# Second attention's tiles: two additions in a row on GpSimd, low keys on VectorE

## What is computed

```python
def _apply_rope(x):
    rot = jnp.stack((-xr[..., 1], xr[..., 0]), axis=-1).reshape(x.shape)
    return x * jnp.cos(ang) + rot * jnp.sin(ang)
...
x = x + 0.5 * ffn0(ln(x)); x = x + attn0(ln(x)); x = x + 0.5 * ffn0(ln(x))
x = x + 0.5 * moe1(ln(x)); x = x + attn1(ln(x)); x = x + 0.5 * moe1(ln(x))
# attn1: q, k, v = split(x @ W_qkv.T); q, k = rope(q), rope(k)
#        softmax(causal(q @ k.T / 4)) @ v, then @ W_o.T
```

## Time and profile before

| what | us |
|---|---|
| median of the runs (lowest, highest) | 843.3 (840.75, 847.4) |
| profiled execution, its own time | 837.3 |
| its span, first to last instruction | 835.5 |
| R of tile 0 starts; C3 is done | 555.6; 581.0 |
| R of tile 4 starts; C7 is done | 630.2; 657.3 |

### The profile page before, as it was taken

The page is one execution under the profiler, slowest core; times in us unless marked ns, Lnnn a source line. Parts: engine busy times, 40 slices in busy tenths (PEclk is TensorE's granted clock), DMA queues, the critical chain, the costliest instruction groups (busy, mean ns, idle before and its releaser), DMA issues. The chain is left out here.

```text
span 835.5 us, 17560 instructions
## 1 busy us (share of the span) xinstructions
PE 718.3 (86%) x5515; PEld 483.5 (58%) x5515; DVE 628.1 (75%) x1436; ACT 458.0 (55%) x1033; POOL 402.9 (48%) x412
## 2 busy tenths in 40 slices
PE   7898959999979999989898699855897598988985
PEld 3454437777636777755455466433785487545652
DVE  5989878778787778698987577543898596775646
ACT  3444568887757788646423266325574475324541
POOL 4545766767666676358636277424005320331440
PEclk8999989999989999999999799976799598998997
DMA  9999994000000000030001243300000010013324
GB/s 371 328 303 182 241 216 2 0 0 0 1 1 1 0 0 0 1 120 1 1 14 51 77 116 109 133 1 1 1 2 1 18 35 2 2 61 88 115 84 151
DMA packets 64945, 59.07 MB, mean 71 GB/s; under 512 B 29106, under 2 KB 59186, under 8 KB 64370
## 3 DMA queue, kind: packets, MB, share of 16 engines
q1 hardware_dynamic: 60706, 47.85, 23.5%
q0 software_dynamic: 3744, 10.26, 3.5%
q10 hardware_dynamic: 432, 0.15, 0.1%
HBM read 27.92 MB, written 30.33 MB: 70 GB/s over the span
## 5 line engine op out<-in xcount | busy, mean ns | idle before, releaser
L1504 PE MATMUL PS<-XT,WA 128*128 128x512 f16 x432 | 101.2, 382 | 0.0
L611 POOL TENSOR_TENSOR ARENA<-ARENA,ST 128x512 f32<-128x512 f32 x64 | 66.6, 1040 | 65.5 <-DVE ST L1284 65.5
L729 ACT ACTIVATE ARENA<-T 128x512 f16<-128x512 f32 (+1 forms) x56 | 35.2, 628 | 109.2 <-DVE T L1162 101.7
L1504 PE MATMUL PS<-WA,ARENA 128*128 128x256 f16 (+2 forms) x960 | 68.4, 213 | 12.7 <-DVE ARENA L1171 11.7
L1504 PEld LDWEIGHTS PS<-WA,ARENA 128*128 128x128 f16 x960 | 56.6, 97 | 29.0 <-DVE ARENA L1171 17.6
L570 POOL DMA_INDIRECT yt_rows<-WA,DIX x46 | 45.4, 987 | 55.0 <-ACT WA L861 41.0
L1504 PEld LDWEIGHTS PS<-XT,WA 128*128 128x128 f16 (+1 forms) x432 | 42.6, 99 | 44.9 <-issue 2.1
L1264 DVE TENSOR_REDUCE ST<-PS 128x2 f32<-128x512 f32 x64 | 44.0, 687 | 27.7 <-PE PS L1504 26.7
L1504 PE MATMUL PS<-KVR,ARENA 128*128 (+1 forms) x384 | 58.2, 280 | 7.5 <-DVE ARENA L1256 4.6
L1504 PE MATMUL PS<-XT,WC 128*128 128x512 f16 x264 | 62.3, 387 | 2.4 <-DVE T L1155 1.4
L762 ACT ACTIVATE ARENA<-PS,ST 128x256 f32<-128x256 f32 x128 | 59.3, 470 | 7.0 <-DVE ST L1267 6.8
(11 more groups left out here) (184 smaller groups left out, 1799.5 us busy)
## 6 DMA issues: line engine op xcount, KB each, us to landing
xs_rows<-ROUT SPq DMA_DIRECT2D x2, 9252.0 KB, 45.9
WA<-xs_rows SPq DMA_DIRECT2D x46, 129.0 KB
WB<-wb_dram SPq DMA_DIRECT2D x1, 4096.0 KB, 21.6
WC<-wc_dram SPq DMA_DIRECT2D x1, 2304.0 KB, 27.3
WA<-wa_dram SPq DMA_DIRECT2D x4, 512.0 KB, 7.3
WA<-wa_dram SPq DMA_DIRECT2D x1, 2048.0 KB, 12.9
WA<-yt_rows SPq DMA_DIRECT2D x4, 512.0 KB, 4.1
WB<-yt_rows SPq DMA_DIRECT2D x4, 512.0 KB, 6.0
```

What stands on the lines that cost most here:

```text
L611: pl.tensor_tensor(pr, pr, rs.broadcast_to([P, 2, S]), ALU.mult).then_inc(norm_done, 1)
L729: sc.activation(HH[r, a, 0, :], T3[r, :], ACT.Copy).then_inc(hid_hi, 1)
L1504: ins = te.matmul(dst, left(a), right(b), start=first and n == 0, stop=last and n == 2, skip_group_check=True)
```

## The change

GpSimd's list now takes the tiles in pairs: add of both tiles, then the low queries of both. The subtraction for the low keys goes to VectorE, as two instructions of 128x256 numbers in place of GpSimd's one of 128x512. `qk1_lo` is split into `q1_lo` (one count for each tile, by GpSimd) and `k1_lo` (two for each tile, by VectorE). VectorE waits for `q1_lo` of tile t-2 before R of tile t; TensorE waits for both before T. The low queries wait for HQ alone, no longer for HK. VectorE's list is written out anew for both halves.

```diff
-            def qk1_low(t, a):
-                pool.wait_ge(qk1_hi, 2 * t + 2)
+            def q1_low(t, a):
+                pool.wait_ge(qk1_hi, 2 * t + 1)
...
-                pl.tensor_tensor(k4[:, :, 1, :, :], t4[:, H1:].broadcast_to([P, H1, 2, DH1]),
-                                 k4[:, :, 0, :, :], ALU.subtract).then_inc(qk1_lo, 1)
...
-            for i in range(TPH):
-                rotated1(i, i % 2)
-                qk1_low(i, i % 2)
+            for i in (0, 2):
+                for t in (i, i + 1):
+                    rotated1(t, t % 2)
+                for t in (i, i + 1):
+                    q1_low(t, t % 2)
...
+            def k1_low(t, a):
+                dve.wait_ge(qk1_hi, 2 * t + 2)
+                t4 = T1[:, a, :].rearrange("p (h o n) -> p h o n", o=1, n=DH1)
+                k4 = QK1[:, a, H1:, :].rearrange("p h (s c n) -> p h s c n", c=2, s=2)
+                for c in range(2):
+                    v.tensor_tensor(k4[:, :, 1, c, :], t4[:, H1:, 0], k4[:, :, 0, c, :], ALU.subtract).then_inc(k1_lo, 1)
...
                 dve.wait_ge(kz_zero, 4)
...
+                rotate(0, 0)
+                values1_low(0, 0, 0)
+                rotate(0, 1)
+                low(0, 0)
+                values1_low(0, 1, 1)
+                low(0, 1)
+                copies1(0, 0, 0)
+                rotate(0, 2)
+                values1_low(0, 2, 2)
+                copies1(0, 1, 1)
+                low(0, 2)
+                rotate(0, 3)
+                values1_low(0, 3, 3)
+                copies1(0, 2, 2)
+                low(0, 3)
+                copies1(0, 3, 3)
                 half(0)
 
-                rotate(0)
+                rotate(1, 0)
                 turn_low(5, 0)
                 values1_low(1, 0, TPH)
-                rotate(1)
+                rotate(1, 1)
+                low(1, 0)
                 values1_low(1, 1, TPH + 1)
+                low(1, 1)
                 turn_stats(6, 0)
                 copies1(1, 0, TPH)
-                rotate(2)
+                rotate(1, 2)
                 values1_low(1, 2, TPH + 2)
                 turn_norm(6, 0)
                 copies1(1, 1, TPH + 1)
-                rotate(3)
+                low(1, 2)
+                rotate(1, 3)
                 values1_low(1, 3, TPH + 3)
                 turn_low(6, 0)
                 copies1(1, 2, TPH + 2)
+                low(1, 3)
                 routing_ranks(6, 0)
                 copies1(1, 3, TPH + 3)
...
             def turn_qk(hf, t, a):
-                pe.wait_ge(qk1_lo, 2 * t + 2)
+                pe.wait_ge(q1_lo, t + 1)
+                pe.wait_ge(k1_lo, 2 * t + 2)
```

More of the change, by code:

```diff
@@ L250, in macaron @@
         qk1_in, v1_in, v1_hi, v1_lo = sem("qk1_in"), sem("v1_in"), sem("v1_hi"), sem("v1_lo")
-        rope1_mul, rope1_sum, qk1_hi, qk1_lo = (sem(n) for n in ("rope1_mul", "rope1_sum", "qk1_hi", "qk1_lo"))
+        rope1_mul, rope1_sum, qk1_hi = (sem(n) for n in ("rope1_mul", "rope1_sum", "qk1_hi"))
+        q1_lo, k1_lo = sem("q1_lo"), sem("k1_lo")
         qk1_turned, q1_copied, k1_copied = sem("qk1_turned"), sem("q1_copied"), sem("k1_copied")
@@ L631, in rotated1 @@
                 pl.tensor_tensor(T1[:, a, :], T1[:, a, :], T2[:, a, :], ALU.add).then_inc(rope1_sum, 1)
-            def qk1_low(t, a):
-                pool.wait_ge(qk1_hi, 2 * t + 2)
+            def q1_low(t, a):
+                pool.wait_ge(qk1_hi, 2 * t + 1)
                 t4 = T1[:, a, :].rearrange("p (h o n) -> p h o n", o=1, n=DH1)
                 q4 = QK1[:, a, 0:H1, :].rearrange("p h (c s n) -> p h c s n", c=2, s=2)
-                k4 = QK1[:, a, H1:, :].rearrange("p h (s c n) -> p h s c n", c=2, s=2)
                 pl.tensor_tensor(q4[:, :, :, 1, :], t4[:, 0:H1].broadcast_to([P, H1, 2, DH1]),
-                                 q4[:, :, :, 0, :], ALU.subtract).then_inc(qk1_lo, 1)
-                pl.tensor_tensor(k4[:, :, 1, :, :], t4[:, H1:].broadcast_to([P, H1, 2, DH1]),
-                                 k4[:, :, 0, :, :], ALU.subtract).then_inc(qk1_lo, 1)
+                                 q4[:, :, :, 0, :], ALU.subtract).then_inc(q1_lo, 1)
             turn(0, 0)
@@ L666, in _ @@
             turn(4, 0)
-            for i in range(TPH):
-                rotated1(i, i % 2)
-                qk1_low(i, i % 2)
-            turn(4, 1)
[L671 to L674, removed]
+            for i in (0, 2):
[3 more added lines that the diff above has]
+                    q1_low(t, t % 2)
+            turn(4, 1)
+            for i in (0, 2):
+                for t in (i, i + 1):
+                    rotated1(TPH + t, t % 2)
+                for t in (i, i + 1):
+                    q1_low(TPH + t, t % 2)
+                if i == 0:
                     turn(6, 0)
@@ L1412, in half, with rotate, low @@
                             turn_low(4, 1)
-                def rotate(i):
-                    dve.wait_ge(qk1_lo, 2 * (TPH + i) - 2)
-                    rotate1(1, i, TPH + i)
-                dve.wait_ge(kz_zero, 4)
[L1419 to L1425, removed]
+                def rotate(hf, i):
+                    t = TPH * hf + i
+                    after(dve, q1_lo, t - 1 if i >= 2 else TPH * hf)
+                    rotate1(hf, i, t)
+                def low(hf, i):
+                    k1_low(TPH * hf + i, i % 2)
+                dve.wait_ge(kz_zero, 4)
+                rotate(0, 0)
[14 more added lines that the diff above has]
+                copies1(0, 3, 3)
                 half(0)
-                rotate(0)
+                rotate(1, 0)
                 turn_low(5, 0)
                 values1_low(1, 0, TPH)
-                rotate(1)
+                rotate(1, 1)
+                low(1, 0)
                 values1_low(1, 1, TPH + 1)
+                low(1, 1)
                 turn_stats(6, 0)
                 copies1(1, 0, TPH)
-                rotate(2)
+                rotate(1, 2)
                 values1_low(1, 2, TPH + 2)
```

## The result

The changed kernel's median is 846.2 us (six runs, 845.3 to 847.6), the kernel before's on the same chip 841.35 (six runs, 840.6 to 847.4). The ratio is 1.0053, 95% interval 1.0032 to 1.0073: slower by half a per cent, where 4.9 us, or 0.6%, was forecast. The profiled execution took 847.55 us, its span 845.7.

The account below looks back on a forecast made before the run. Both preparations of tiles were taken as chains of latency with no engine full. The chains' +1.4 and +3.5 gave +4.9 us on the median of 843.3, so 848 us, with an 8-in-10 range of 840.5 to 853.

Parts of the forecast that it names:

- T2: TensorE's transposes of tile 2, behind low queries that stand behind tile 3's addition: start 2.4 us later.
- first chain: From R of tile 0 to the last copy of tile 3: 1.4 us longer, bounds -0.4 and +2.1.
- T6: TensorE's transposes of tile 6, behind tile 7's addition and the low queries: start 4.2 us later.
- second chain: From R of tile 4 to the last copy of tile 7: 3.5 us longer, bounds +1.0 and +5.5.
- Premise: Both preparations of tiles: no engine is full, only chain length counts, and every microsecond passes to the kernel's end.
- Tiles 0 and 1: First half: low keys' two halves meet GpSimd's addition and low queries; tile 0's transposes start 0.2 us later, no gain.
- Tiles 2 and 3: First half: tile 3's R waits behind low keys, low queries behind its addition; transposes 2.4 and 1.15 us later.
- Tiles 4 to 7: Second half: low keys delay statistics and the copy of tile 4's keys by 4.4 us; chain end 3.5 us later.
- the rival of the falling clock: Second-half products and more loop steps run at TensorE's low clock: +4.3 on +4.9 us, 852.5 us; chance 0.17.
- The price of a meeting: VectorE and GpSimd at SBUF: VectorE ends 0.29 us behind GpSimd's instruction, which grows by 0.28 us.
- The rival without meetings: Low keys on VectorE neither block nor are blocked; only order costs, +1.5 us, 844.8 us; chance 0.13.
- A faster GpSimd would have won nothing: At tile 1's transposes: the products ahead on TensorE run until 566.58, so they can't come before.

Follow-up runs that it names:

- e10: The changed kernel run once more, on another chip; ratio 1.0051 against the kernel before.
- e8: The kernel before with ten unused chained VectorE multiplications ahead of the last copy of the first half; ratio 1.0062 against the kernel before.
- e2: The changed kernel with GpSimd's additions and low queries tile by tile again, low keys still on VectorE; ratio 1.0034 against the kernel before.
- e1: The changed kernel with VectorE's low keys of tiles 2 and 6 behind the next tile's R, tile 5's behind the statistics; ratio 1.0023 against the kernel before.
- e4: The changed kernel with the low keys as one VectorE instruction of 128x512 numbers, not two halves; ratio 1.0052 against the kernel before.
- e3: The changed kernel with the low keys' place filled with zeros by two memsets that read nothing; ratio 1.0005 against the kernel before.
- e12: The kernel before with one wait changed: low queries wait for HQ alone, low keys still on GpSimd wait for HK; ratio 0.996 against the kernel before.
- e5: The changed kernel with GpSimd's order and VectorE's places for low keys both undone, low keys still on VectorE; ratio 0.9988 against the kernel before.
- e9: The kernel before with e5's lists for tiles 0 to 3, and low queries waiting for HQ alone in tiles 4 to 7; ratio 0.9965.

## Why the prediction was right

The order of events and the sign were right, and the sum's two terms were each within 0.5 us. That the sum came out to a tenth is luck. One profile of the changed kernel gives +4.8 for the two chains, e10's gives +2.8; with the products at the full level on both sides it is about 1.4 + 2.2 = +3.6 (25.96 against some 24.6, and e10's 29.26 against 27.03), which also lies in the measured interval of 2.7 to 6.1 us. The absolute time was 846.2 and not 848, as the kernel before's median fell from 843.3 to 841.35 with three more runs.

| step | forecast | measured |
|---|---|---|
| T0 | +0.2 | +0.4 |
| R3 | +1.5 | +1.6 |
| T2 | +2.4 | +2.5 |
| T3 | +1.15 | +1.8 |
| first chain | +1.4 | +1.8 |
| T4 | +1.6 | +1.4 |
| copy of tile 4's keys | +4.4 | +4.1 |
| T5 | +3.5 | +3.1 |
| add6 | +1.9 | +1.4 |
| T6 | +4.2 | +4.7 |
| T7 | +2.9 | +2.9 |
| second chain | +3.5 | +3.0 |

*Premise: both preparations are chains of latency, and every microsecond passes on.* Right for C3 by e8. The table of experiments agrees: the chains' sum lies in the measured interval of every kernel but e2; these intervals are 3 to 6 us wide.

*Tiles 0 and 1.* Right in kind: KL0's halves met add1 and QL0 as written, and T0 started 0.14 us behind KL0. The extra 0.2 is R1, which waited for its product and ended 3.62 after R0 and not 3.42.

*Tiles 2 and 3: KL2 ahead of R3, add3 ahead of QL2.* Right, and the largest step. e1 takes the first away, e2 the second, and either brings T2 forward, to 17.6 and 14.9 after R0. T2 took 1.87 us at the low clock in place of 1.38; this 0.5 us, which the prediction named and took in by half, and 0.1 at T2's start make T3 1.8 late where 1.15 was forecast, and C3 with it. So the order's term was right and the clock's was too small.

*Tiles 4 to 7.* Right: the additions to X behind KL5, the copy at +4.1. Two sizes were off. The meetings were a little cheaper: add5 took 1.37 where 1.27 + 0.28 was forecast. And T6's lateness came another way at its end: R7 was released by QK7, which with V7 ran for 4.05 us at the low clock, not by KL6. That is the place that the rival of the falling clock named. In e10, with every start up to R6 within 0.1 us of the same place, QK7 and V7 took 2.65 us, R7 stood behind KL6 at 18.09 after R4 and not 18.84, T6 at 21.98 and not 22.76, and C7 ended at 29.26 and not 30.04. So the low clock cost 0.8 us at T6 and the same at C7. What gave it back against the forecast is T6 itself, 1.05 us where the kernel before's took 1.86, so that KL7 was done earlier than forecast though T6 had started later. The two slips of 0.8 cancel, and that too is luck. The rival's other half, more slow steps in the loops, shows in the second loop, where five of the shift's steps took 0.80 us or more against three before; but two of the five stand right behind the pause of 5.3 us, so they can't be put on the change. The first loop had three and before four. One figure of the rival was off in itself: with T4 at 638.2, V6 ends near 641.2 and not 641.5. The ranks took 3.1 us, from 659.37 to 662.5, as forecast (3.3), for they had no GpSimd beside them.

*The price of a meeting.* In the trace KL takes 1.4 to 1.8 us a tile with one meeting, 2.63 with two, 0.74 to 0.76 with none, so "ends 0.29 behind the GpSimd instruction" fits. "GpSimd grows by 0.28" was misread. An instruction doesn't grow because the other engine starts under it: add1 took its plain 1.26 with KL0 begun 0.22 behind it. It grows when it starts under a running one, by what is left of that less 0.13 to 0.16: add5 started with 0.26 left of KL4's first half (0.42 from 639.07) and grew by 0.10, add1 of e4 with 0.52 left of 0.68 and grew by 0.37. VectorE's 0.29 behind is the same, 0.42 less 0.13. The pairs of QL grew by 0.37 and 0.43 for two such starts, where I had 0.28 for each. The Trainium skill ("SBUF — State Buffer", section "Who interferes with whom") has an exclusive lock on the shared port and lets whoever starts second block fully (it says "fully blocks" of VectorE's 2-port modes, and that two operands in SBUF contend as well); the rows agree but for that 0.13 to 0.16 at the handover, and my sentence that it would be 0.42 each time overlooked that only what is left counts. The rival without meetings falls by KL's rows. Its own price was off too: it put +1.5 us on the orders alone, and e3 has +0.2.

*What was missed: the wait for HQ alone.* The prediction went through the orders and KL's price and gave the third edit, QL's shorter wait, no line at all. In the changed kernel it is worth nothing to the first QL of a pair, and so the sum was right: QL0 started at 563.33 when add1 ended, HK0 had ended at 562.29; QL2 at 576.28 behind add3, HK2 at 572.9. By itself it is worth 2.0 us in the second chain and about 2.1 in the first at an equal clock (22.54 against some 24.6), and 0.4% of the time. The change hid its own best part behind the pairing.

*"A faster GpSimd would have won nothing" at T1.* Wrong. In the profile that it was read from, KL1 ended at 566.59 and the products at 566.58, so the two tied, by the low clock of the products. In e8, with the same lists and the products at 2.11 us, T1 waited for KL1:

```profile
567.09 1.05 PE L1800 MATMUL PS<-IDH,ARENA 128*128 128x128 f16 x16 [1.83 <-POOL ARENA L641]
```

And the products stand behind T0, which waits for GpSimd. In e12 T0 came 0.5 us earlier, the products with it, and T1 at 10.13 was held by C0 only. It cost the forecast nothing, as KL was done in time for T1 in the changed kernel.

*The rule that elementwise work belongs on VectorE.* The Trainium skill ("GPSIMD Engine Reference", section "Engine selection") puts such work on VectorE, GpSimd being about 2x slower with two inputs; with the prediction's own rows that was 2.5 us for eight KL. KL alone is shorter on VectorE, 0.76 for 1.15, which is 1.5 times and not 2. But e5, which has the move and the shorter wait without the bad orders, stands at 0.9988, and e12, which has the shorter wait and no move, at 0.996. The intervals overlap, so the times don't settle it. The chains say that the move costs more than it saves once QL no longer waits for HK. T0, ahead of QK2 and its clock, stands at 6.43 in e5 and 5.77 in e12. The second chain took 27.41 in e5 and 25.03 in e9, which has e5's first half and KL of tiles 4 to 7 on GpSimd.

*What stays open.* What the pause of 5.3 us is, and why R0 came 2.8 us later. And e2's median: its profiled execution was 2.3 us under the median of its runs (834.47 against 836.72), e4's 3.1 and e5's 3.0 under theirs, so a chain read from one execution can flatter its kernel by about as much as is at stake. What sets the clock's level at the products was not varied on purpose.

## What to carry to other kernels

In a chain of latency look for the instruction that is ready and stands behind one that is not: putting two of a kind in a row holds back the first one's consumer until the second one's input has come, and a short instruction ahead of a waiting one hands on its own wait. Before work is moved to a faster engine, ask of each wait whether its semaphore counts more than the operand that is read; GpSimd's idle time of the earlier trace rows, 1.26 us a tile ahead of QL, was such a wait, and by the chains shortening it beat moving the work. And an edit that is worth nothing in the kernel at hand because another edit hides it still needs its line in the sum, or the part worth keeping is thrown away with the rest.

## What of the hardware was not expected

- In these runs it mattered who starts first, and not whether the work was cut in two. A VectorE instruction of 128x512 that began 0.16 us ahead of GpSimd's took 0.68 and stretched the other from 1.26 to 1.63; one that began under GpSimd took 1.50. Two of 128x256 under two GpSimd instructions in a row took 2.63, against 0.76 alone: the engines took strict turns, and the two didn't slip in together at one gap. At each handover 0.13 to 0.16 us overlap.
- The same program met either clock level at the same place in different executions: 3.62 and 2.11 us for twelve products, with 1.2 us at the end of the chain. The low level fell on these products or on those before them, as R1's time shows.
